# Another set of pace constants for a merged order of nine kinds of work on one core

## The reference

```python
h = layernorm(x) * (1 + ca) + sa
x = x + ga * (local_attention(h) + scatter(heavy_attention(routed rows of h)))   # window 64, 8 heads of 64
h = layernorm(x) * (1 + cb) + sb
x = x + gb * small_mlp(h)              # 64 units, each its own 16 relu units
h = layernorm(x) * (1 + ca') + sa'
x = x + ga' * causal_attention(h)      # 16 heads of 16, rope, a norm on every query and key
h = layernorm(x) * (1 + cb') + sb'
x = x + gb' * mlp(h)                   # 256 -> 1024 -> 256, gelu
```

## Time and profile before

| | |
|---|---|
| median of 3 runs | 4180.76 us (4180.42 to 4183.39) |
| the profiled execution | 4184.49 us, its span 4182.8 us |
| PE busy | 3493.0 us, 84% of the span |
| DVE, ACT, POOL busy | 58%, 46%, 36% |
| mean granted TensorE clock | 0.910 of full speed |
| one element in the middle | about 484 us |

### The profile page before, as it was taken

One profiled execution on the slowest core, in us unless ns is written; L12 is line 12 of the kernel. 1 busy time (PEld: TensorE's weight loads), 2 busy tenths in 40 slices (PEclk: granted clock), 3 DMA queues, 4 the chain that ended last, 5 costly groups with the idle time before them and its releaser, 6 DMA issues. The chain is left out here.

```text
span 4182.8 us, 81798 instructions
## 1 busy us (share of the span) xinstructions
PE 3493.0 (84%) x30905; PEld 2016.8 (48%) x30905; DVE 2443.1 (58%) x6156; ACT 1921.3 (46%) x4521; POOL 1502.2 (36%) x1807
## 2 busy tenths in 40 slices
PE   6378779987799778997799878997889987998787
PEld 2245444554446544465446544465445654465444
DVE  6755757366663657456573665546573565736662
ACT  5124426454265444544264443554445442644433
POOL 4223442353333452244423542334512444235311
PEclk8589889998899989998899988998999988999889
DMA  7210230001300231002300113002300023001220
GB/s 237 73 36 14 62 107 15 25 20 47 104 19 21 54 89 40 15 14 61 107 15 25 31 48 92 27 12 54 103 26 15 22 53 107 15 25 31 47 67 6
DMA packets 233602, 207.38 MB, mean 50 GB/s; under 512 B 13776, under 2 KB 214224, under 8 KB 233176
## 3 DMA queue, kind: packets, MB, share of 16 engines
q1 hardware_dynamic: 229168, 192.61, 16.6%
q0 software_dynamic: 3328, 8.39, 0.7%
q10 hardware_dynamic: 720, 1.15, 0.1%
HBM read 123.83 MB, written 77.69 MB: 48 GB/s over the span
## 5 line engine op out<-in xcount | busy, mean ns | idle before, releaser
L2369 ACT ACTIVATE arena<-pb 128x512 f32<-128x512 f32 (+3 forms) x1536 | 665.2, 494 | 249.9 <-PE pb L1595 242.8
L2449 POOL TENSOR_TENSOR arena<-arena,small 128x512 f32<-128x512 f32 x256 | 287.9, 1127 | 455.5 <-DVE small L1771 454.1
L2198 ACT ACTIVATE arena<-arena,small 128x256 f32<-128x256 f32 x512 | 256.0, 500 | 402.7 <-DVE small L1754 396.8
L1595 PE MATMUL pb<-arena 98*32 98x512 bf16 (+3 forms) x4608 | 404.7, 347 | 18.1 <-ACT arena L2369 11.4
L1613 PE MATMUL pb<-arena,v 128*17 128x512 f32 (+3 forms) x3072 | 382.1, 502 | 39.1 <-POOL arena L2613 29.3
L1553 PE MATMUL pb<-arena 96*32 96x128 bf16 (+5 forms) x5280 | 365.4, 274 | 57.8 <-DVE arena L2053 28.3
L2613 POOL TENSOR_SCALAR_AFFINE_SELECT arena<-arena 128x256 f32<-128x256 f32 x512 | 217.7, 427 | 484.5 <-ACT arena L2369 481.2
L2053 DVE TENSOR_REDUCE arena<-pb 128x1 f32<-128x512 f32 x512 | 333.9, 685 | 78.5 <-PE pb L1553 76.6
L1754 DVE CUSTOM_DVE_ANT_0 arena<-pb,wmask 128x256 f32<-128x256 f32 x512 | 195.8, 420 | 213.0 <-PE pb L1290 212.8
L1553 PEld LDWEIGHTS pb<-arena 96*32 96x32 bf16 (+1 forms) x5280 | 180.6, 99 | 257.7 <-issue 74.1
L1290 PE MATMUL pb<-arena 128*128 128x256 f32 x1024 | 282.4, 401 | 5.2 <-issue 4.5
(11 more groups left out here) (332 smaller groups left out, 6971.0 us busy)
## 6 DMA issues: line engine op xcount, KB each, us to landing
arena<-split_q SPq DMA_DIRECT2D x64, 384.0 KB, 4.3
arena<-split_k SPq DMA_DIRECT2D x24, 768.0 KB, 6.7
split_q<-arena SPq DMA_DIRECT2D x64, 192.0 KB, 2.3
split_q<-arena SPq DMA_DIRECT2D x96, 128.0 KB, 2.0
split_k<-arena SPq DMA_DIRECT2D x64, 192.0 KB, 2.4
split_k<-arena SPq DMA_DIRECT2D x96, 128.0 KB, 2.1
arena<-split_k SPq DMA_DIRECT2D x24, 384.0 KB, 6.0
xn<-h_d SPq DMA_DIRECT2D x8, 1024.0 KB
```

The costliest lines, as they stand in the source:

```text
L1595: mm = t.matmul(bank[bk][r:r + 32, 0:w_], ka[slot(c, g)][0:KA, h, kt_ * P + r:kt_ * P + r + 32], qa[slot(c, g)][0:KA, h, q0:NH], start=Tru ...
L2198: ins = s.activation(pm[n % 3][:, j], sm[n % 2][:, j], ACT.Exp, bias=nmx[:, 2 * sl + j:2 * sl + j + 1], scale=-1.0, accum_out=sml[:, 2 * s ...
L2369: s.activation(pp[pn % 4][:, h % 2, 0:w_], bank[n % 3][:, 0:w_], ACT.Exp).then_inc(a_exp1, 1)
L2449: g.tensor_tensor(pm[n % 3], pm[n % 3], rcl[:, 2 * sl:2 * sl + 2].unsqueeze(2).broadcast_to([P, 2, 2 * P]), ALU.mult).then_inc(p_norm0, 1)
```

## The change: constants of the schedule

No operation is added or removed. Only the order changes in which steps of the three lanes are merged. The constants:

```diff
-PACE = {('light', 0): (1.88, 0.9), ('light', 1): (1.0, 1.1), ('att', 0): (1.79, 0.9, 0.72), ('att', 1): (1.0, 1.15, 0.72)}
+PACE = {("light", 0): (1.88, 0.9, 0.9), ("light", 1): (1.0, 1.463, 1.1), ("att", 0): (1.461, 0.9, 0.9, 0.72), ("att", 1): (1.0, 1.15, 1.15, 0.632)}
+
+SIDE = {("chain", 0): 1.0, ("chain", 1): 1.0, ("chain", 2): 1.0, ("chain", 3): 1.0, ("heavy", 0): 1.0,
+        ("mlp1", 0): 1.0, ("mlp1", 1): 0.98, ("hrows", 0): 1.0, ("hnorm", 0): 1.0}
...
-HROWS_BEHIND_MLP, HEAVY_BEHIND_HROWS, HEAVY_BEHIND_ATT, HNORM_BEHIND_ATT, ATT_BEHIND_MLP, MLP_BEHIND_LIGHT = (9, 12, 15, 46, 14, 2)
+HROWS_BEHIND_MLP, HEAVY_BEHIND_HROWS, HEAVY_BEHIND_ATT, HNORM_BEHIND_ATT, ATT_BEHIND_MLP, MLP_BEHIND_LIGHT = (6, 12, 11, 45, 13, 2)
 LOAD_STEP = 8
-LAG = 14
+LAG = 11
...
     if key[0] == "light":
-        return (PACE if key[1] else FIRST)[key[0], key[2]][n >= (17, 12)[key[2]]]
+        f = (17, 12)[key[2]]
+        if key[1] == 0:
+            return FIRST[key[0], key[2]][n >= f]
+        return PACE[key[0], key[2]][(n >= f) + (n >= f + UNITS)]
     if key[0] == "att":
-        f = len(first_fills(key[2])) + 1
-        return PACE[key[0], key[2]][(n >= f) + (n >= f + NG * TH * (key[2] + 1))]
+        f, g = len(first_fills(key[2])) + 1, NG * TH * (key[2] + 1)
+        return PACE[key[0], key[2]][(n >= f) + (n >= f + g // 2) + (n >= f + g)]
...
             if lanes[lane]:
+                key = lanes[lane][0]
+                due[lane] += SIDE[key[0], key[2]] if key[1] or key[0] != "chain" else 1.0
+            while due[lane] >= 1.0 and lanes[lane]:
                 turn(lane)
+                due[lane] -= 1.0
```

More of the change, by code:

```diff
@@ L132, in schedule @@
     gate["hrows", 0, 0] = [(("begin", 0, 0), 1)]
-    order, done, lag, credit, pace = [], {}, {}, 0.0, 1.0
+    order, done, lag, credit, pace, due = [], {}, {}, 0.0, 1.0, [0.0, 0.0, 0.0]
     def reached(wants):
```

## The result

The changed kernel takes 4112.73 us in the median of four runs (4108.54 to 4113.75), the kernel before 4182.08 us beside it (4180.42 to 4184.59). The ratio is 0.9832, with a 95% interval of 0.9815 to 0.9849. So the sign and most of the named waits were right, but 4151 was forecast and the range ended at 4119.

The account below looks back on a forecast made before the run. PE was taken to bound the kernel, busy 3493.0 of 4182.8 us. Terms of -24.8 us over 8 elements and -4.9 over 7 gave -29.7, from 4180.8 to 4151 us; range 4119 to 4193, its own core 4134 to 4170.

Parts of the forecast that it names:

- Where the time goes: Whole kernel: PE busy 3493.0 of 4182.8 us at mean clock 0.91; only its idle or half-speed time can come back.
- Waits that the change can't reach: PE's 8 us at the start of att(b, 0) and 5 us ahead of mlp1(b, 0): both stay, 0.
- a): Units of light(b, 1) at 1.463: more independent PE work passes each long DVE operation; -2.1 us an element.
- Rival 4: Stretch 1998 to 2026: half of its 1.2 GHz time returns to 2.4 GHz, 2.8 us an element more, 4129; chance 0.08.
- b): First maxima of att(b, 0) at 1.461: 12 rounds instead of 10, no clear surplus on PE or DVE; 0, within 1 us.
- c): End of att(b, 0) and chain(b, 3): a projection covers a wait, -2.0, exposed projections cost +1.0; net -1.0 us an element.
- rival 1: End of att(b, 0): DVE sets the pace and it gets slower, 4197 us; chance 0.20.
- d): Entry of att(b, 1), with mlp1(b, 0) and heavy(b+1): shorter PE waits, less three added heavy steps; -1.2 us an element.
- e): Tail of att(b, 1): heavy ends 8 rounds before it instead of 3, less work between transposes and projections; +0.5 us an element.
- The stage named as a sign: First maxima of att(b, 1) to heavy's first projection: 1.5 to 2 us shorter if the forecast is right.
- Rival 2: PE's waits only move, the next late copy making it wait instead: 4179 us; chance 0.14.
- Rival 3: Light(b, 1): POOL's scaling stretches DVE's two-input operations, 2.1 us an element, cancelling the gain there, 4168; chance 0.13.

Follow-up runs that it names:

- e1: The kernel before with the first 16 unit steps of light(b, 1), b > 0, at 1.463 a round instead of 1.1: 4138.84 us beside 4180.39, ratio 0.9896.

## Why the prediction was right and wrong

**Where the time goes.** Right that only idle and half-speed time could come back, and that PE's busy time would stay within 1% (it fell by 0.6%); but the sum priced idle time alone. The reading then took element 3 as the pattern. Its units were the shortest of the seven (69.5 us; the others 70.3 to 75.1), and its scores ended up only 0.5 us shorter, where the mean is 2.7. So one element hid both large terms: elements 5 and 7 gave 9.7 and 8.7 us in the units alone.

**Waits that the change can't reach.** Held: the gap to att(b, 0) and the wait ahead of mlp1(b, 0) moved by -0.2 and +0.2 us an element.

**a) Mechanism right, size wrong.** Forecast -2.1 an element, the trace has -4.2. The waits went nearly as costed: idle time fell by 1.3 an element. The term that was missing is the time at 1.2 GHz in the units, 68.3 us over seven elements before and 17.1 after; PE's busy time in the units went down by 20.0 us with it. It isn't the luck of two traces: the other kernels with the rate of 1.1 have 51 to 68 us at half clock there, those with 1.463 have 0 to 34. Rival 4 had this mechanism, and priced it at 2.8 us an element, but placed it at the end of the scores and in the tail of att(b, 0), and gave it 0.08. The tail has 6.0 us more of half-clock time over seven elements; the scores have 20.5 less, but only 4.5 us less of busy time. The Trainium skill, TensorE: Matmul & The Clock Gate, section The HAM clock gate, says that sustained work raises the clock, and the row of light(5, 1), 0.89 before and 1.00 after, agrees. The experiment with the extra matmuls is too close to the spread of executions to bound this. A caution on the size: a alone gave 42 us, but taking it out of the change cost 9, so "-4.2 an element" is what the trace of this combination shows in this piece, not the worth of the edit. The sum also took a for eight elements, while the new rate holds for seven, which is 2.1 us too much.

**b) The failed step: "0, within 1 us either way".** It was priced by the stretch in which the maxima run, and there it held nearly (+0.6 an element). But two rounds more in this stretch move chains 2 and 3 by two steps, in places three, against everything of att(b, 0) behind it. Alone that was worth 43 us, in the change 49: the largest part, and with an offset alone 18.1 us came back in the scores and the tail, of the 40.2 that b gives there. What the forecast put at nothing without a reason is this effect on the scores, which are 19.2 us shorter in the change and 30.1 with b alone. What it relieves is partly POOL, where the mask stood behind rotations and a bias; with a part of these left out, 13 us came back. The row that told of it, 29.3 us in 21 pieces of up to 4.6, stood in the view of waits from which the earlier trace rows were taken, between two rows that were used. The rest isn't settled: b also cleared DVE's L2033 at the end of the chain, and shortened waits for ACT's exp with b alone (24.3 to 17.8 us; in the changed kernel they are 28.4), and no run separates these.

**c) Right, and somewhat better.** Forecast -1.0 an element, the trace has -2.0 in the tail. The wait at L1529 was costed at -2.0 and fell by 11.5 / 8 = 1.4. The price, a quarter of two exposed projections, +1.0, didn't show. So rival 1, DVE setting the pace there, fell. c belongs to b, though: with a alone that wait stays at 18.0 us, with b alone it is 4.6. And the shorter tail is no proof of c: with a alone it is 17.5 us shorter with the wait still there.

**d) and e) Near in their sum, not in their parts.** Forecast -4.9 over seven elements; mlp1's first matmuls, the maxima, scores and tail of att(b, 1) sum to -2.8. The stage named as a sign, maxima to heavy's first projection, got no shorter: the maxima, which begin earlier and share PE with mlp1, are 2.4 us longer an element, and mlp1 before them 1.7 shorter. That the sum came near is partly luck. DVE does wait longer for the gathers, as was feared (70.3 us in the changed kernel, 43.9 before), and what the two steps fell short of their forecast is 2.1 us over seven elements; whether that is it no run shows. But inside the change the gates are worth 18 us, mostly in other stages. LAG was costed at 0: alone it is 0, in the change some 7.

**Rivals.** Rival 2, that waits only move, fell for the whole; for the tail in e1, with 17.5 us gained and 18.2 lost right behind, it is exactly what happened. Rival 3, contention, isn't seen in the changed kernel. Line L1998 of the earlier trace rows, now L2008:

```profile
L2008 DVE TENSOR_TENSOR arena<-arena x64: 664/684/1226, 433.6 to 3901.1; 128x512 f32<-128x512 f32 x64
```

The median is the same 684 ns and the longest is 1226 in place of 1751. With a alone the median is 822 ns, and that kernel was 42 us faster all the same. The stretching exists, then, and it goes with the order; what it cost in time no run separates.

**What the sum itself got wrong.** It added parts. Alone they sum to 100 us, together they give 69, a and b together no more than either, and one taken out costs 49 or 9. A fractional rate leaves a remainder of credit, which takes part in the pairing of the pieces behind it, so an edit doesn't stay in its stage. The range was built from each step's own bounds, and had no term for this, nor for a stage downstream. Its lower end isn't what it says either: two thirds of the bounds of a, c and d give 4130, and 4119 takes some 0.8 of them.

## What to carry to other kernels

When an edit changes how many rounds a stage takes, price the stages behind it too: list, for the slow side engines, what will stand ahead of the operation for which PE waits, and start from the rows of long waits in pieces, over all elements and not over one. Count time at half clock beside idle time, since closing gaps can return more through shorter matmuls than through the waits themselves. In an order merged by fractional rates, set the remainder at the start of each stage deliberately and try some values; a constant tuned without that can be good by chance. And don't expect measured parts to add up.

## What the runs showed of the hardware

- The same 352 matmuls took 63.92 us at a granted clock of 0.89, with 11.1 us of idle time among them, and 56.79 us at 1.00 with 8.6. The longest single pause in them was 3.3 us in the one and 1.5 us in the other. The sum of idle time alone doesn't tell the clock: with 7.4 us of it the clock was 0.95, with 10.7 us it was 0.98.
- Extra matmuls of 15 us raised PE's busy time by 7.7 us, and the median by 8.6. In that trace the units had 20.5 us less at half clock; that this is the reason isn't shown.
- POOL's 128x256 product with a table takes 0.75 to 0.77 us in some places and 1.18 to 1.19 us in others, for the same form (L2586 and L2587, later L2596 and L2597, in the timelines above).
- Holding back the loads of the second and third group shortened the wait for the first by less than 1 us of 7 in each element. That speaks for loads served nearly in their order and against an even share.
